# Moving the transposed norms behind both value products of the second token tile, and the third group ahead of the slot's attended product

## The reference, cut to what matters

```python
q, k, v = l2norm(x @ Wq), l2norm(x @ Wk), l2norm(x @ Wv)      # 16, 16 and 64 columns a head
attn = jnp.square(jax.nn.relu(einsum('bhid,bhjd->bhij', q, k)))
out = einsum('bhij,bhjd->bhid', attn, v)
n = norm(out)                                                  # of each token and head
out = tanh(n) * out / maximum(n, 1e-12)
x = x + merge_heads(out) @ Wout
```

## Time and profile before

| | us |
|---|---|
| median of 3 timed runs | 558.39 |
| the three runs | 556.79, 558.39, 560.27 |
| the profiled execution, its own time | 556.18 |
| its span from first to last instruction | 554.2 |

### The profile page before, as it was taken

How to read it: one execution, slowest core, us unless ns; L and a number is a source line. 1 busy time by engine, 2 the same in 40 slices (tenths; PEclk the granted TensorE clock), 3 DMA queues, 4 the chain that set the end, 5 groups by cost and what they waited for, 6 DMA issues and landing times.

```text
span 554.2 us, 10167 instructions
## 1 busy us (share of the span) xinstructions
PE 528.0 (95%) x3304; PEld 400.8 (72%) x3304; DVE 425.1 (77%) x1004; ACT 372.2 (67%) x674; POOL 331.7 (60%) x280
## 2 busy tenths in 40 slices
PE   7789799999999997899999999999999999999997
PEld 6455557676666665686878878888888888888874
DVE  5886878888979687669779779779778778777675
ACT  5697758777878875454475865865865865755644
POOL 6655829384855654386466756556556555665563
PEclk9999989999999999999999999999999999999999
DMA  7401010101010104900191760940870951851920
GB/s 217 130 2 29 2 30 1 31 1 30 2 31 1 30 2 130 194 0 2 56 218 37 178 148 18 220 104 15 184 145 11 220 110 30 204 116 47 215 66 19
DMA packets 36099, 44.73 MB, mean 81 GB/s; under 512 B 5456, under 2 KB 18896, under 8 KB 36048
## 3 DMA queue, kind: packets, MB, share of 16 engines
q1 hardware_dynamic: 31360, 42.40, 33.0%
q10 hardware_dynamic: 4688, 1.71, 1.3%
HBM read 40.94 MB, written 3.15 MB: 80 GB/s over the span
## 4 chain that ended last, share of the span: by engine, by line
PE 78%; issue 6%; DVE 6%; POOL 4%; ACT 4%; DMA 1%; SPq 0%; ACTq 0%; DVEq 0%; POOLq 0%
PE PS L1224 75%; POOL hl L505 3%; DVE aT L869 1%; ACT v L546 1%; ACT rl L571 1%; DMA Osb<-wa_dram 1%; DVE n L848 1%; PE PS L1345 1%; PE PS L1359 1%; POOL v L421 1%; POOL vi L461 1%; DVE nmx L881 0%; ACT sqv L553 0%; PE PS L1487 0%; PE PS L1317 0%
## 5 line engine op out<-in xcount | busy, mean ns | idle before, releaser
L505 POOL TENSOR_TENSOR hl<-hb,hh 128x512 fp32r<-128x512 f32 x127 | 164.3, 1295 | 129.1 <-ACT hh L712 127.8
L705 ACT ACTIVATE sil<-PS 128x512 f32<-128x512 f32 (+1 forms) x136 | 80.8, 594 | 82.3 <-PE PS L1224 81.6
L1091 DVE TENSOR_TENSOR PS<-sil,PS 128x512 f32<-128x512 f32 x128 | 88.3, 690 | 58.2 <-PE PS L1224 36.6
L1224 PE MATMUL PS<-fxh,wfh 128*128 128x512 f32 x264 | 104.4, 395 | 2.9 <-issue 1.7
L1224 PE MATMUL PS<-fxl,wfh 128*128 128x512 f32 x264 | 104.0, 394 | 0.0
L1224 PE MATMUL PS<-fxh,wfl 128*128 128x512 f32 x264 | 103.8, 393 | 0.0
L712 ACT ACTIVATE hh<-hb 128x512 fp32r<-128x512 f32 x128 | 80.3, 627 | 30.7 <-DVE hb L1096 26.3
L1096 DVE TENSOR_TENSOR hb<-PS,wbc 128x512 f32<-128x512 f32 x128 | 88.5, 691 | 9.6 <-DMA wbc<-w_dram 2.8
L869 DVE SCALAR_TENSOR_TENSOR aT<-PS,rl 128x1024 f32<-128x1024 f32 x64 | 75.2, 1216 | 14.8 <-ACT rl L571 14.5
L571 ACT ACTIVATE rl<-PS 128x1024 f32<-128x1024 f32 x64 | 62.8, 1049 | 23.5 <-PE PS L1224 23.5
L425 POOL TENSOR_TENSOR sr<-n2o,half 128x32 f32<-128x32 f32 x7 | 37.9, 5421 | 49.2 <-DVE n2o L876 49.2
(11 more groups left out here) (179 smaller groups left out, 911.7 us busy)
## 6 DMA issues: line engine op xcount, KB each, us to landing
wbc<-w_dram SPq DMA_DIRECT2D x48, 512.0 KB, 11.1
wbc<-w_dram SPq DMA_DIRECT2D x32, 128.0 KB, 2.9
wbc<-w_dram SPq DMA_DIRECT2D x16, 256.0 KB, 4.2
wfs<-wf_dram SPq DMA_DIRECT2D x32, 98.0 KB, 2.1
band_dram<-zero SPq DMA_DIRECT2D x16, 80.0 KB, 1.7
band<-band_dram ACTq DMA_DIRECT2D x4, 320.0 KB, 3.0
X<-x_dram SPq DMA_DIRECT2D x1, 896.0 KB, 8.3
Osb<-wa_dram SPq DMA_DIRECT2D x3, 256.0 KB, 4.0
```

The costliest lines, as they stand in the source:

```text
L505: g.tensor_tensor(hl[:, n % RING, :], hb[:, n % RING, :], hh[:, n % RING, :].bitcast(F32), ALU.subtract).then_inc(F("hl"), 1)
L705: s.activation(sil[0:rows, n % 2, :], PS[0:rows, G0 + n % 2, :], ACT.Silu).then_inc(F("silu"), 1)
L1091: v_.tensor_tensor(PS[:, bank, :], sil[:, n % 2, :], PS[:, bank, :], ALU.mult).then_inc(F("t"), 1)
L1224: return nc.tensor.matmul(o, w, m, start=start, stop=stop)
```

## The change

Two things change their place, with no instruction added or taken away.

- `transpose_norms(q)` stood between `values(n, 1, 0)` and `values(n, 1, 1)` on TensorE; it now stands behind both. The table of turns is changed with it, so that nt and v(n, 1, 1) change their PSUM banks with each other. With that g(n, 0) waits for the bank of v(n, 1, 1) and g(n, 1) for that of nt, where it was the other way round.
- `group(n, 2)` stood behind `attend(4b + 2)` on TensorE; it now stands ahead of it, behind the two other groups. On ScalarE `keep_group(n, 2)` goes ahead of `keep_output(4b + 2)`. Its place in the table of turns is as before.

```diff
--- before.py
+++ after.py
@@ -96,7 +96,7 @@
         n, q, r = b + 1, b - 1, b - 2
         order += late(r, ("F", r, 2), ("F", r, 3))
         order += coming(n, ("qk", n, 0), ("qk", n, 1), ("v", n, 0, 0), ("v", n, 0, 1)) + late(q, ("nb", q))
-        order += coming(n, ("v", n, 1, 0)) + late(q, ("nt", q)) + coming(n, ("v", n, 1, 1))
+        order += coming(n, ("v", n, 1, 0), ("v", n, 1, 1)) + late(q, ("nt", q))
         order += ([("px", 0)] if b == B - 2 else []) + ([("pc", 0)] if b == B - 1 else []) + late(r, ("y", r, 0))
         order += coming(n, ("g", n, 0), ("g", n, 1), ("g", n, 2))
         order += coming(n + 1, ("xT", n + 1)) + late(q, ("ft", q)) + late(r, ("y", r, 1))
@@ -675,9 +675,8 @@
                     square_values(n, 1)
                     keep_group(n, 0)
                     keep_group(n, 1)
+                    keep_group(n, 2)
                 keep_output(NG * b + 2)
-                if more:
-                    keep_group(n, 2)
                 if b:
                     tanh_norms(q)
                 weight_high(NG * b + 2)
@@ -1407,10 +1406,9 @@
                 score(NG * b + 2)
                 if more:
                     values(n, 1, 0)
+                    values(n, 1, 1)
                 if b:
                     transpose_norms(q)
-                if more:
-                    values(n, 1, 1)
                 attend(NG * b + 1)
                 if b == B - 2:
                     prep_transpose(0)
@@ -1423,9 +1421,8 @@
                 if more:
                     group(n, 0)
                     group(n, 1)
+                    group(n, 2)
                 attend(NG * b + 2)
-                if more:
-                    group(n, 2)
 
                 score(NG * b + 4)
                 if n + 1 < B:
```

## The result

| | before | after |
|---|---|---|
| median of 22 timed runs each, us | 558.55 | 561.70 |
| lowest and highest, us | 555.47, 562.66 | 558.95, 564.38 |
| ratio, with its 95% interval | | 1.0051 (1.0030 to 1.0071) |
| profiled execution, us (span) | 556.18 (554.2) | 560.80 (558.8) |

The changed kernel is 3.15 us slower by the medians, 0.5%. The forecast was +3.3 us. In the experiments a few executions took 590 to 2888 us; the ratios leave them out, while the medians contain them and would be up to 0.6 us lower without them.

What follows compares the result with a forecast made beforehand. Predicted bound: the path from `nt` through GpSimd, held floor `nm` and `xTl` to F(q, 0), TensorE at most 0.29 us behind. 2.8 + 0.4 + 0.1 = +3.3 us on the mean 557.9 gives 561.2 us, range 557.5 to 564.5.

Steps and rivals of the forecast that it cites:

- The path: From `nt` through GpSimd, held floor `nm`, `Fpad` and `xTl` to F(q, 0); TensorE's stream at most 0.29 us behind.
- Four batches at 0.7 us: b = 2 to 5: later `nt` delays the scaling, `nm` and F(q, 0); four times 0.7 = 2.8 us.
- Batch 6: No tokens to transpose; some 0.3 us slack ahead of the factors' transpose, so 0.7 less 0.3 is 0.4 us.
- Batch 1: `nmx` starts 0.3 us before the scaling, not held; product f is held instead, to about 63.4: +0.1 us.
- Rival D: Only b = 1 differs: `nmx` is caught, +0.6 us, 561.8 us; chance 0.67 together with the forecast.
- The third group: g(n, 2) ahead of the attended product, b = 0 to 6: no wait, spares at most 0.2 us a batch, taken as 0.
- The sum: Whole kernel: 2.8 + 0.4 + 0.1 = +3.3 us, giving 561.2 us from the four executions' mean.
- A: At F(q, 0): TensorE's stream bounds the batch, only the spared switch remains, 1.4 us less, 556.5 us; chance 0.15.
- B: No effect: the 0.7 us are taken up by an overlooked pause, 558 us; chance 0.13.
- C: Much slower by the clock: new waits bring the lower clock into b = 2 to 6, 16 us, 574 us; chance 0.05.

Runs made afterwards that it cites:

- the repeated run with the late GpSimd: Kernel before, TensorE untouched, one small GpSimd power added ahead of `sr` in b = 1 to 6, run again: 561.89 us, ratio 1.0058.
- the new order on GpSimd: Kernel before, GpSimd making both powers and small products first, then both scalings: 554.54 us, ratio 0.9928; same order in the changed kernel: 555.00 us.
- The version with the third group moved: Kernel before with GpSimd's powers and small products ahead of both scalings, and g(n, 2) ahead of the attended product: 554.26 us, again 553.77 us.

## Why the prediction was right

*The path.* Predicted: the batch is closed by `nt`, GpSimd's series, the held floor, `Fpad`, `xTl`, F(q, 0), with TensorE at most 0.29 us behind. Shown: lateness put in on GpSimd alone costs the same as the moved `nt`, and without the hold the moved `nt` costs nothing. The room was 0.14 to 0.17 us.

*Four batches at 0.7 us.* Measured 0.69 us each (26.76 for 26.07), 107.05 us from the `nt` of b = 2 to that of b = 6 and not 104.33: +2.72 us for 2.8.

*Batch 6.* `nt` to `ft` went from 13.72 to 13.37 us; with the 0.70 by which `nt` itself is later that is +0.35 us for 0.4.

*Batch 1.* `nmx` slipped ahead, the product f was held, as forecast. From `nt` to the end of `Fpad` 12.28 us and not 12.90, and with the 0.70 of `nt` +0.08 for 0.1. The whole distance to the next `nt` can only be compared where the low stretch in it is alike: 28.79 us in the repeated run with the late GpSimd, 28.74 before. Rival D, `nmx` caught, falls with its 0.12 us.

*The third group.* No wait was added, and the attended product takes 1.88 us up to the scores that follow it directly, as it took up to the third group before. With the new order on GpSimd the scores start 10.18 us after `nt` with the group moved and 10.37 us with it in its old place, so 0.19 us are spared. That it is the switch of the array's shape that costs them is inferred from the order of the jobs. Counted at 0 in the sum, and it was 0 (26.08 us alone). It became worth 0.2 us a batch only when the hold was gone.

*The sum.* +3.3 forecast, +3.15 by the medians, within the 1.7 to 4.0 us of the interval. The steps as the traces show them, 2.72 + 0.35 + 0.08, give 3.15 as well; that the medians agree with them so closely is luck, as the interval is 2.3 us wide. Rivals A and B fall by the steady distance of 26.76; C too, as the granted clock is 1.00 from 81 to 205 us in the changed kernel. The new waits, each under 1 us, brought no low stretch there.

*One gain was mostly not what it seems*, that of GpSimd's new order: 2.0 us expected, 3.8 by the medians. At an equal granted clock it is 1.2 to 1.5 us, so the expectation was rather too high. The rest is that these executions spent less time at the lower level: their mean granted clock is 0.9945 over 11 executions, and 0.989 over the 76 of the kernel before. In the trace the `nt` of b = 2 came 25.07 us behind that of b = 1 where it was 28.74 before. I had 1.3 us there for `nmx`. The version with the third group moved took 25.05 us there in one execution, with no low stretch, and 27.96 in the other, with one as long as before. So of the 3.67 us some 2.9 go with the low stretch and some 0.8 at most with `nmx`; the four steady batches add 0.66. The 39 executions of all versions with the new order have a mean granted clock of 0.993, so fewer low stretches are no accident of one trace. The pause of TensorE's matmuls in b = 1 is 1.3 to 1.4 us in them and 1.9 before; whether this shorter pause is the cause stays open, as two of their four traces have a low stretch behind it all the same.

## What to carry to other kernels

A long product of GpSimd on SBUF, as the scaling here, is also a lock on parts of VectorE's work: moving what triggers it moves the lock. A small operation that takes three to thirteen times its usual time, ending within 0.05 us of GpSimd's, is how the lock shows. GpSimd's powers, though longer, held none of these operations. Look at what VectorE has to do in that window, and put GpSimd's long products where VectorE's operations take an input from PSUM, as here behind the factors. And when a change moves a step back by some tenths, follow what hangs on it round to where it meets the main stream: 95% busy time said nothing of it, the pause at the meeting point did.

## What the runs showed of the hardware that was not expected

The same kernel on the same input has stretches of some 3 to 7 us at a lower granted clock that come in some executions and not in others, near 20, 45, 70 and from 222 to 231 us. TensorE's matmuls pause for 1.3 to 2.1 us shortly ahead of these places in every execution, with or without the stretch. One of them cost 2.6 us in the case above. They make most of the spread of the timed runs (7 us from the lowest to the highest of 22), which is twice the effect studied here. Two readings get round them. The distance between two equal instructions in the undisturbed part of a trace repeats to 0.04 us, and timed executions can be compared at an equal granted clock.
